# A causal attention on one core: a tile's output product leaves PSUM by ScalarE and is added up by GpSimd, where VectorE added it straight from PSUM

## The reference, cut to what matters

```
def _L2_ffn_ref(x, ln_w, ff_ln_w, wq, wk, wv, wo, wg, w1, w3, w2):
    B, S, D = x.shape                       # seen as 1, 1024, 256
    h = _rms(x, ln_w)
    q = (h @ wq).reshape(B, S, 32, 64)
    k = (h @ wk).reshape(B, S, 8, 64)
    v = (h @ wv).reshape(B, S, 8, 64)
    q, k = _rope(q, k)
    k, v = repeat(k, 4), repeat(v, 4)
    scores = einsum('bqhd,bkhd->bhqk', q, k) / 8
    attn = softmax(where(causal, scores, -1e30))
    o = einsum('bhqk,bkhd->bqhd', attn, v)
    x = x + o @ wo
    ...
```

## Time and profile before

| what | value |
|---|---|
| median of 3 runs | 4028.41 us (4026.26 to 4034.68) |
| the profiled execution's own time | 4031.66 us |
| its span, first to last instruction | 4029.8 us |
| busy share of the span | PE 85%, DVE 61%, ACT 49%, POOL 41% |
| granted TensorE clock, mean | 0.923 of full speed |
| the two attention stages | about 1045 to 1776 us and 2662 to 3387 us of the span |

### The profile page before, as it was taken

How to read it: one execution, slowest core, us unless ns; L and a number is a source line. 1 busy time by engine, 2 the same in 40 slices (tenths; PEclk the granted TensorE clock), 3 DMA queues, 4 the chain that set the end, 5 groups by cost and what they waited for, 6 DMA issues and landing times. The chain is left out here.

```text
span 4029.8 us, 59505 instructions
## 1 busy us (share of the span) xinstructions
PE 3425.7 (85%) x18336; PEld 2687.8 (67%) x18336; DVE 2462.0 (61%) x4855; ACT 1960.6 (49%) x3926; POOL 1666.5 (41%) x1286
## 2 busy tenths in 40 slices
PE   5788697589888888879986888888888887998979
PEld 4566585268566666658865777756666665887867
DVE  4677554944677777765455333357777776545554
ACT  3777434333566666653333222146666665333333
POOL 1665121922566666632203333156666663221211
PEclk8999898999899999999987777789999999999989
DMA  2000231432111000013310000011100001332222
GB/s 79 18 27 3 83 110 58 141 97 88 54 27 27 22 22 22 21 42 119 109 34 5 0 0 0 10 52 27 28 23 22 22 21 42 119 111 81 88 84 76
DMA packets 81041, 202.86 MB, mean 50 GB/s; under 512 B 16923, under 2 KB 20123, under 8 KB 80662
## 3 DMA queue, kind: packets, MB, share of 16 engines
q1 hardware_dynamic: 80774, 201.26, 16.1%
q10 hardware_dynamic: 144, 0.07, 0.0%
HBM read 171.39 MB, written 4.69 MB: 44 GB/s over the span
## 5 line engine op out<-in xcount | busy, mean ns | idle before, releaser
L1209 POOL TENSOR_TENSOR probs<-probs,row_inverse 128x640 f32<-128x640 f32 (+7 forms) x640 | 733.1, 1147 | 596.4 <-DVE row_inverse L1235 579.0
L548 PE MATMUL psUp<-xnT_part,weights_part 128*128 128x512 f32 x3456 | 839.6, 393 | 3.3 <-POOL weights_part L522 1.3
L548 PEld LDWEIGHTS psUp<-xnT_part,weights_part 128*128 128x128 f32 x3456 | 634.3, 189 | 124.8 <-POOL weights_part L522 3.3
L525 POOL TENSOR_TENSOR weights_part<-weights,weights_part 128x768 fp32r<-128x768 f32 x136 | 250.9, 1848 | 1025.1 <-ACT weights_part L598 1025.1
L1223 DVE TENSOR_REDUCE neg_max<-psS 128x1 f32<-128x640 f32 (+7 forms) x640 | 477.2, 746 | 165.5 <-PE psS L1114 165.0
L1192 ACT ACTIVATE probsT_part<-psT 128x512 fp32r<-128x512 f32 (+1 forms) x960 | 439.9, 489 | 274.0 <-PE psT L1126 272.5
L1250 DVE TENSOR_TENSOR probsT_part<-psT,probsT_part 128x512 fp32r<-128x512 f32 (+1 forms) x960 | 505.2, 551 | 101.5 <-ACT probsT_part L1192 85.1
L1126 PE MATMUL psT<-ident,probs 128*128 128x128 f32 x2880 | 453.0, 280 | 109.1 <-DVE probsT_part L1250 83.7
L1176 ACT ACTIVATE probs<-psS,neg_max 128x640 f32<-128x640 f32 (+7 forms) x640 | 474.2, 741 | 77.1 <-DVE neg_max L1223 72.4
L559 PEld LDWEIGHTS psDown<-weights_part,hidden_part 128*128 128x128 f32 x3456 | 457.9, 195 | 56.3 <-issue 23.3
L559 PE MATMUL psDown<-weights_part,hidden_part 128*128 128x256 f32 x3456 | 468.2, 287 | 31.2 <-DVE hidden_part L709 31.2
(11 more groups left out here) (317 smaller groups left out, 4973.0 us busy)
## 6 DMA issues: line engine op xcount, KB each, us to landing
gates<-gate_rows SPq DMA_DIRECT2D x136, 512.0 KB, 4.0
weights<-in_l_ffn SPq DMA_DIRECT2D x148, 384.0 KB, 4.4
qk_swapped<-qk_raw SPq DMA_DIRECT2D x384, 64.0 KB, 2.0
bc_broadcast<-bc_rows SPq DMA_DIRECT2D x32, 512.0 KB, 4.4
w_group<-in_l_wgroup SPq DMA_DIRECT2D x16, 384.0 KB, 3.2
q_whole<-q_steps SPq DMA_DIRECT2D x32, 128.0 KB
w_o_group<-in_l_wo SPq DMA_DIRECT2D x16, 256.0 KB, 2.7
rope<-in_l_rope SPq DMA_DIRECT2D x2, 1024.0 KB, 5.7
```

The lines of the kernel that those rows point to most:

```text
L525: nc.gpsimd.tensor_tensor(w[1][:, j, :], wt[:, j, :], w[0][:, j, :].bitcast(F32), ALU.subtract).then_inc(w_split, 1)
L548: last = nc.tensor.matmul(psU[:, u % 2, g, :], wp[:, j, g * D + k * P:g * D + (k + 1) * P], xp[:, k, cols(half)], start=n == 0, stop=n == ...
L1209: self.nc.gpsimd.tensor_tensor(self.p[:, n % 4, 0:w], self.p[:, n % 4, 0:w], self.rinv[:, at:at + 1].to_broadcast([P, w]), ALU.mult).then_ ...
```

## The change

The output product of a tile takes two hops to `acc` instead of one. ACT copies `share` to one half of a new SBUF buffer `out_part`, in its own step order behind all that it does in that step, and this copy lets the next user have the bank. POOL adds that half to `acc`, behind all that it does in that step. ACT waits, before it overwrites a half, for the addition two tiles back (`out_added`, which starts at two). DVE has nothing of it any more, and at the stage's end waits for POOL's last addition.

```diff
+        self.out = s.sb("out_part", [P, 2, D])
...
+        self.out_added = s.sem("out_added_plus_two")
...
@@ act_step
+        if kind == "output" and s >= 0:
+            act.wait_ge(self.share_ps, self.jobs_before(g, s, last) + 1)
+            act.wait_ge(self.out_added, NT * g + u + 1)
+            self.nc.scalar.activation(self.out[:, u % 2, :], self.share[:, 0:D], ACT.Copy).then_inc(self.share_read, 1)
@@ pool_step
         super().pool_step(pool, g, s, last)
+        kind, j = self.job(s, last)
+        if kind == "output" and s >= 0:
+            pool.wait_ge(self.share_read, self.jobs_before(g, s, last) + 1)
+            t = GroupAttention.ORDER[j]
+            self.nc.gpsimd.tensor_tensor(self.acc[:, t, :], self.out[:, j % 2, :], self.acc[:, t, :],
+                                         ALU.add).then_inc(self.out_added, 1)
@@ dve_step
-        dve.wait_ge(self.share_ps, self.jobs_before(g, s, last) + 1)
-        t = GroupAttention.ORDER[j]
-        self.nc.vector.tensor_tensor(self.acc[:, t, :], self.share[:, 0:D], self.acc[:, t, :],
-                                     ALU.add).then_inc(self.share_read, 1)
@@ l2_attention
+            pool.sem_inc(hooks.out_added, 2)
             att.pool(pool, G)
...
-            dve.wait_ge(hooks.share_read, hooks.jobs_before(G - 1, T, True))
+            dve.wait_ge(hooks.out_added, NT * G + 2)
```

More of the change, by code:

```diff
@@ L1606, in dve_step @@
         kind, j = self.job(s, last)
-        if kind is None or s < 0:
-            return
-        if kind == "project":
+        if kind == "project" and s >= 0:
             self.rotate(dve, g + 1, j, self.share[:])
-            return
-        dve.wait_ge(self.share_ps, self.jobs_before(g, s, last) + 1)
-        t = GroupAttention.ORDER[j]
-        self.nc.vector.tensor_tensor(self.acc[:, t, :], self.share[:, 0:D], self.acc[:, t, :],
-                                     ALU.add).then_inc(self.share_read, 1)
 def l2_attention(core):
```

## The result

| what | before | after |
|---|---|---|
| median of 4 runs each | 4027.3 us (4019.9 to 4034.7) | 4068.8 us (4064.9 to 4071.7) |
| ratio, 95% interval | | 1.0107 (1.0088 to 1.0125) |
| the profiled execution's own time | 4031.7 us | 4066.9 us |
| its span | 4029.8 us | 4064.9 us |
| the 14 groups that prepare a next one | 1249.5 us | 1280.7 us |

The loss is 41 us by the medians, where the prediction had 22 and a range that ended at 4067. Of the 35 us between the two profiled executions 31 lie in the 14 groups, measured from a group's first output product to the next one's.

What follows compares the result with a forecast made beforehand. PE was taken to set the pace, its idle time per group (10.7 us) counting. Step 20's 11.8, steps 24 to 31's 6.2, ACT's 2.3 and the stage ends' 1.5 made 21.8 us over 4028.4: 4050 us, range 4036 to 4067.

Steps and rivals of the forecast that it cites:

- Bound and place: PE sets the pace and twice in each group stands behind POOL, whose order now has the additions ahead.
- Step 20, 0.84 us: POOL's addition, after waiting for ACT's copy, makes the split queries and PE 0.84 us late in 14 groups: 11.8 us.
- Steps 24 to 31, 0.44 us: POOL's further additions delay its multiplications and the maximum in step 31 by 0.44 us in 14 groups: 6.2 us.
- no wait would shrink by more than 0.3: Sign to look for: in PE's idle time no wait for POOL or DVE shrinks by more than 0.3 us.
- ACT's shifts (2.3): ACT's copies delay what is queued behind them: 0.1 us per group, 0.45 per last group of a stage, 2.3 us.
- the ends of the stages (1.5): Behind each stage's last product a copy, addition and signal replace DVE's addition: 0.73 us more, twice, 1.5 us.
- The clock: Rival, chance 0.13: PE's longer wait before step 24 drops its clock in 7 more groups, 17 us on top, 4067 us.

Runs made afterwards that it cites:

- late20_shift: Changed kernel with 45 counting instructions on ACT ahead of the second stage, four buffer slots, POOL's step 20 addition moved to step 30: 4022.2 us, 0.9999.
- dummy20_before: Kernel before plus a POOL addition of two 128x256 tables into an unused buffer in step 20 of the 14 groups: 4028.0 us, 0.9995.
- dose256_before: Kernel before plus a dummy 128x256 POOL addition at the end of step 21 in the 14 groups: 4055.5 us, 1.0065.
- shift_after: Changed kernel with 45 instructions on ACT ahead of the second attention stage that only count up an unused semaphore: 4066.1 us, 1.0113.
- late_pad: Changed kernel, unshifted, four buffer slots, POOL's additions of a group's last four tiles moved to steps 30 and 31 in the 14 groups: 4038.5 us, 1.0033.
- shift_before: Kernel before with 45 instructions on ACT ahead of the second attention stage that only count up an unused semaphore: 4017.3 us, 0.9983.
- add23_before: Kernel before with DVE's addition of the fifth tile's product moved from step 20 to step 23: 4020.9 us, 0.9984.

## Why the prediction missed

- **Bound and place: right.** PE waits for POOL's split queries, with the addition in POOL's order ahead of them, and late20_shift, which moves that addition, is level with the kernel before.
- **Step 20, 0.84 us: nearly right.** It measured 0.72 on POOL and 0.7 from product to product at full clock; PE's wait went to 2.32, forecast about 2.3. That POOL waits for ACT's copy first was in the working; dummy20_before showed that without this wait the addition costs nothing.
- **Steps 24 to 31, 0.44 us: not found as a cost of its own.** From step 28's product to step 31's it is 9.78 us in the one group with full clock there, for 9.25 to 9.28 in the second stage of before, which is the size forecast. But over all 14 groups this stretch grew by 2.3 us only, with 6 us more of it at 1.2 GHz, and PE's idle time in it fell by 1.6. PE's wait for DVE in step 31 shrank from 1.57 to 1.05, since DVE got in between the addition and the multiplication, where the prediction said that no wait would shrink by more than 0.3. And late20_shift keeps these additions and loses nothing.
- **ACT's shifts (2.3) and the ends of the stages (1.5): small at most.** The last groups did not change (56.4 us each), where 0.45 each was allowed; the ends of the stages were not told apart.
- **The clock: the step that failed.** The sum was made at equal clock, and a lower clock stood beside it as a rival with 0.13 and 4067 us. It is what happened: 12 slowed stretches for 6, where the rival assumed 7 more than before. The prediction's argument against it was that some groups had kept full speed at a wait of 1.87 us. Dose256_before shows what 0.60 us more do: of 27 us of loss 18 are clock. By that dose step 20's term was some 27 us, and not the 11.8 of the sum, which priced a delay at its own length.
- **The reload of ACT's loop: missed.** Nothing of it was in the prediction. In the changed kernel's trace it is 8 us of PE's idle time, but without it (shift_after) the measured time is lower by no more than the interval; in late_pad it makes 10 to 12.
- **What is left.** Shift_after, which has no reload, is 42.6 us above the kernel before, and the dose of 0.60 us explains 27 of them (by its interval 19 to 33). The other 16 or so go too when step 20's addition is moved (late20_shift), so they hang on it. Its delay is 0.70 us and not 0.60, which may be part of them, but no experiment took them apart, and the profiled execution of shift_after, 7 us under its median, shows only part of them.

## What to carry to other kernels

Where one engine sets the pace and its clock is seen to drop in some rounds and not in others, a delay on its path is priced by its length times a factor that a run with a dummy delay can show; here it was about 1 for 0.34 us (0 to 2 by the interval) and about 3 for 0.60 (2 to 4). A slow engine's extra work is free where it fills a wait, so look at what it must wait for first: moving one addition from behind a late copy to a place behind the critical splits gave back the whole loss. And look at the instruction queue when a change adds to a loop or to what stands ahead of it, since a loop that showed no transfers may be fetched anew in each round; whether that costs anything depends on whether the engine's stall reaches the one that sets the pace.

## What the runs showed of the hardware

- A loop of 325 instructions on ACT showed no transfer on the instruction queue in one place of the program and five of 8 KB per round in another (0.73 MB in 89 transfers in the whole program), with ACT standing 3.04 us at the return (changed kernel). 45 instructions ahead of it took them away (shift_after), and brought five per round to a loop of 301 (shift_before), where PE's idle time at the return stayed within 0.15 us of what it was.
- The same stretch of work took 11.87 us at full clock and 14.38 with part of it at 1.2 GHz (shift_after). With a dummy delay of 0.60 us per group PE's time at 1.2 GHz in 14 groups went from 82 to 126 us, and its busy time for the same work from 1094 to 1116 us (dose256_before).
- Two splits of 128x512 that meet on DVE and POOL took 0.68 and 1.70 us with DVE first by 0.13 us (the kernel before), 1.14 and 1.55 with DVE first by 0.74 (the changed kernel), and 1.62 and 1.28 with POOL first by 0.20 (add23_before).
